# A planner that orders TensorE's work by a cost for every new division of the array, and new lengths for the units

## The chip, the cores and the metric

One core of one Trainium2 chip runs the kernel. The metric is the device time in microseconds (us) of the whole program. The median of three runs of the kernel before is 3766.3 us (3763.3 to 3766.73).

## The reference, cut to what matters

```python
x = x + tanh(g_xattn[0]) * L0_xattn(layernorm(x), ctx)      # 16 heads of 64, 1601 keys, batch 4 x 512 x 256
x = x + tanh(g_ffn[0])   * L0_ffn(layernorm(x))             # GQA attention (16 heads of 16), then MoE:
                                                            # 8 experts, top 2, capacity 1280, 256 -> 512 -> 256
x = x + tanh(g_xattn[1]) * L1_xattn(ctx, ctx, layernorm(x)) # queries layernorm(x), 16 heads of 16, masked, 1601 keys
x = x + tanh(g_ffn[1])   * L1_ffn(layernorm(x))             # attention (16 heads of 16) plus 8 dense experts, top 2
```

Every attention is an exact softmax: the row maximum is found first and subtracted, then the scores are exponentiated, then multiplied with the values, and divided by their sum.

## The kernel before, in words

All of the program's work is cut into units: one unit is a few matmuls of TensorE (PE) that fill one buffer of PSUM, and what evicts that buffer. Each engine walks through one common list of units in the same order and does its own share of each, waiting on counters of the others. So the list decides what stands behind what on every engine. PSUM has a ring of three buffers of two banks each (`RING = 3`), and two accumulators (`pv`) beside it. Nearly every unit takes one buffer of the ring; a score unit of the narrow blocks takes two.

The units that matter here, with the letters used below:

- **m**, a maximum: two matmuls of queries on 401 keys each (`maxa`, line 1075, for the wide first block with its heads of 64; `max3`, line 1173, for the third block). VectorE (DVE) reduces the buffer. In `max3` the head sits in 32 of the array's rows, and the next unit's head in the next 32.
- **x**, the same for the second and fourth block (`maxb`, line 1185): two heads, 512 keys each.
- **S**, scores of one tile of 124 keys. In the wide block (`scorea`, lines 1091 and 1094) one buffer, exponentiated by ScalarE (ACT), summed by GpSimd (POOL). In the third block (`scoreb`, lines 1205, 1212, 1218) two buffers: the mask is added by matmuls on all rows before and after, four heads stand in four groups of 32 rows, and the second pair of heads waits for the second buffer only when its turn comes. ACT exponentiates the two halves.
- **P**, exponentials times values into `pv` (`pva` line 1105, column halves of 64; `pvb` line 1233, four column groups of 32). No buffer of the ring.
- **u** and **o**, the sum over keys and the output projection of the wide block (`suma` line 1112, `outa` line 1120), with a chain of five DVE operations between them; **T**, transposes after a layer norm (line 1043); **K**, **V**, **Q**, projections (lines 1052 to 1067); **s**, **r**, **l** (`strip`, `rowb`, `low`, lines 1164 and 1192), one each for a group of four heads: r needs the reduction of all of the group's maxima on DVE.

The list is made on the host. Generators yield `Step`s, each with a length on PE (`pe`), the evictions (`use`), and the number of buffers (`slots`). `Pace` keeps a clock for PE, for each evicting engine and for the three buffers. `weave` merges the generators: it takes the step with the least progress among those that could start within `slack` of the first that could. There are three weaves: the wide block with the second one in it, the experts, and the third block with the fourth in it (called the last stretch below). Where the clocks leave PE idle near the ends, `warmed` puts dummy matmuls (line 1027). The scatter of the rows to the experts (`("scatter", b)`) has no `Step`: it goes into the list behind `ranks`, and POOL issues eight indirect DMAs there.

## Time and profile before

| | us |
|---|---|
| median of three runs | 3766.3 |
| the profiled execution, its own time | 3768.0 |
| its span, first to last instruction | 3766.0 |
| PE busy (share of the span) | 3496.2 (93%) |
| DVE busy | 1984.7 (53%) |
| ACT busy | 1442.6 (38%) |
| POOL busy | 986.3 (26%) |
| chain that ended last, share on PE | 85% |
| mean granted clock of TensorE | 0.956 |

Busy PE is time in which a matmul is under way; matmuls that wait inside a unit for a buffer can lie behind others that are still in flight, so a busy PE is not a full one. Idle time in brackets behind a row is that of the engine just before it, and the arrow names what ended it.

### The profile page before, as it was taken

What the parts mean: (1) busy time and instruction counts of PE and PEld (TensorE: products, weight loads), DVE (VectorE), ACT (ScalarE), POOL (GpSimd) and SP (SyncE); (2) the same over time, 40 slices, a digit from 0 to 9 for tenths busy, and PEclk for the clock granted to TensorE, in tenths of its full rate; (3) what the DMA queues carried; (4) which work ended last, traced back from release to release, by engine and by line L of the source; (5) the groups of instructions that cost most, each with busy time, mean ns of one, the idle gap of its engine ahead of it and who ended that gap; (6) DMA issues with size and microseconds to landing.
All of it is one profiled execution on the core that took longest, in us unless ns stands there. A gap on an engine that the chain in (4) does not pass through costs nothing.

```text
span 3766.0 us, 44527 instructions
## 1 busy us (share of the span) xinstructions
PE 3496.2 (93%) x18489; PEld 1465.0 (39%) x18489; DVE 1984.7 (53%) x3278; ACT 1442.6 (38%) x1645; POOL 986.3 (26%) x481
## 2 busy tenths in 40 slices
PE   7999999989999989999786949899999999999998
PEld 3444434434344443434235712234323422343252
DVE  4444456454554645555251156655666566656244
ACT  3333444434444334443231104443444244434513
POOL 3555355354544545454501030000000000000000
PEclk9999999999999989999898959999999999999999
DMA  3000000000000000000113320211101110110000
GB/s 147 12 12 29 12 6 12 12 35 12 7 12 8 28 23 6 12 2 8 73 32 109 118 56 23 65 27 39 28 23 28 39 28 23 28 39 22 7 13 6
DMA packets 68245, 114.87 MB, mean 31 GB/s; under 512 B 4850, under 2 KB 49546, under 8 KB 67531
## 3 DMA queue, kind: packets, MB, share of 16 engines
q1 hardware_dynamic: 62666, 97.08, 8.1%
q0 software_dynamic: 5376, 14.95, 1.8%
q8 instruction: 145, 2.38, 0.3%
q14 instruction: 58, 0.47, 0.0%
HBM read 101.79 MB, written 16.78 MB: 31 GB/s over the span
## 4 chain that ended last, share of the span: by engine, by line
PE 85%; DVE 7%; ACT 4%; POOL 2%; issue 2%; DMA 1%; another core or an unknown queue 0%; DVEq 0%; ACTq 0%; POOLq 0%
PE ring L1212 11%; PE pv L1105 10%; PE ring L1094 9%; PE pv L1233 9%; PE ring L1173 4%; PE ring L1205 3%; PE ring L1075 3%; PE ring L1218 3%; PE ring L1091 3%; PE ring L1052 3%; PE ring L1066 3%; PE ring L1067 2%; PE ring L1053 2%; PE ring L1291 2%; PE ring L1272 2%; PE ring L1120 2%
## 5 line engine op out<-in xcount | busy, mean ns | idle before, releaser
L1480 POOL TENSOR_TENSOR wide<-wide 124x1024 f32<-124x1024 f32 (+1 forms) x352 | 828.0, 2352 | 268.6 <-ACT wide L1374 254.7
L1381 ACT ACTIVATE wide<-ring 124x1024 f32<-124x1024 f32 (+2 forms) x544 | 530.3, 1023 | 620.2 <-PE ring L1212 615.8
L1374 ACT ACTIVATE wide<-ring 124x1024 f32<-124x1024 f32 (+1 forms) x416 | 425.9, 1025 | 582.3 <-PE ring L1094 547.0
L1615 DVE CUSTOM_DVE_ANT_0 rest<-ring,slim 128x802 bf16<-128x802 f32 x512 | 508.7, 994 | 265.2 <-PE ring L1173 217.3
L1599 DVE TENSOR_REDUCE max_a<-ring 128x2 f32<-128x802 f32 x512 | 508.1, 995 | 242.6 <-PE ring L1075 242.1
L1105 PE MATMUL pv<-wide 124*64 124x512 f32 (+1 forms) x1664 | 453.1, 624 | 25.2 <-ACT wide L1374 25.2
L1094 PE MATMUL ring<-wide 64*124 64x512 f32 (+1 forms) x1664 | 429.0, 594 | 0.0
L1625 DVE TENSOR_REDUCE slim<-ring 128x2 f32<-128x1024 f32 x256 | 309.7, 1223 | 159.2 <-PE ring L1185 156.5
L1212 PE MATMUL ring<-slim 32*128 32x512 f32 x2176 | 383.4, 651 | 5.0 <-DVE slim L1640 3.8
L1450 POOL DMA_DIRECT2D slim<-in_ctx_k x16 | 8.6, 542 | 1079.8 <-PE ring L1173 704.2
L1173 PE MATMUL ring<-slim 32*128 32x401 bf16 x1024 | 233.9, 356 | 38.1 <-DVE max_b L1615 13.2
L1477 POOL TENSOR_TENSOR wide<-wide 124x1024 f32<-124x1024 f32 x32 | 75.3, 2353 | 637.0 <-PE pv L1105 451.8
L1233 PE MATMUL pv<-wide,slim 124*32 124x512 f32 (+1 forms) x1664 | 224.3, 611 | 0.7 <-ACT wide L1381 0.6
L1212 PEld LDWEIGHTS ring<-slim 32*128 32x128 f32 x2176 | 128.5, 186 | 158.9 <-issue 99.4
L1105 PEld LDWEIGHTS pv<-wide 124*64 124x64 f32 (+1 forms) x1664 | 83.7, 136 | 264.9 <-issue 214.3
L1075 PE MATMUL ring<-wide 64*128 64x401 bf16 x1024 | 176.2, 341 | 7.1 <-DVE max_a L1599 5.8
L1091 PE MATMUL ring<-wide,select_b 64*128 64x512 bf16 x832 | 161.0, 384 | 14.1 <-ACT wide L1374 12.1
L1173 PEld LDWEIGHTS ring<-slim 32*128 32x128 bf16 x1024 | 55.7, 94 | 285.6 <-ACT wide L1381 137.1
L1094 PEld LDWEIGHTS ring<-wide 64*124 64x124 f32 (+1 forms) x1664 | 157.7, 186 | 22.3 <-issue 2.9
L1589 DVE CAST wide<-wide 128x800 bf16<-128x800 f32 x64 | 37.1, 579 | 244.5 <-ACT wide L1351 174.7
L1066 PE MATMUL ring<-wide 128*124 128x128 f32 (+1 forms) x832 | 160.1, 274 | 0.0
L1067 PE MATMUL ring<-wide 128*124 128x128 f32 (+1 forms) x832 | 159.5, 272 | 0.0
(236 smaller groups left out, 4120.0 us busy)
## 6 DMA issues: line engine op xcount, KB each, us to landing
slim<-in_ctx_k SPq DMA_DIRECT2D x16, 800.5 KB, 4.3
wide<-in_w_pair SPq DMA_DIRECT2D x32, 384.0 KB, 3.1
slim<-in_ctx_v SPq DMA_DIRECT2D x16, 744.0 KB
wide<-in_w SPq DMA_DIRECT2D x16, 512.0 KB, 4.9
wide<-in_we SPq DMA_DIRECT2D x16, 512.0 KB, 3.8
wide<-in_ctxT SPq DMA_DIRECT2D x4, 1601.0 KB, 7.6
slim<-in_ctx_k POOLq DMA_DIRECT2D x16, 400.2 KB, 4.7
wide<-padded_x SPq DMA_DIRECT2D x8, 640.0 KB, 6.5
```

The costliest lines, as they stand in the source:

```text
L1075: last = pe.matmul(slot[:, h * BANK:h * BANK + CHUNK], queries_ab[own, q * P:(q + 1) * P], keys_ab[own, c0:c0 + CHUNK], start=True, stop=True)
L1094: last = pe.matmul(slot[0:kn, h * BANK:(h + 1) * BANK], keys_a[own, p % 2, k0:k0 + kn], queries_a[own, p % 2, :], start=False, stop=True)
L1105: last = pe.matmul(pv_a[64 * h:64 * h + 64, :], values_a[0:kn, p % 2, k, 64 * h:64 * h + 64], exps_a[0:kn, slot_of["scorea", b, p, k], h * ...
L1173: last = pe.matmul(slot[:, j * BANK:j * BANK + CHUNK], queries_low(3, g)[own, q * P:(q + 1) * P], keys_low(3, g)[own, c0:c0 + CHUNK], star ...
L1212: last = pe.matmul(head_bank(unit, h), key_columns(blk, g, k0)[own, :], queries_place(blk, g)[own, :], start=blk != 3 or h >= 2, stop=blk ...
L1233: last = pe.matmul(pv_of[blk][PAD * h:PAD * h + PAD, :], value_columns(blk, g, k, kn, h), exps_tile(blk, b, g, k, h)[0:kn, :], start=k == ...
L1374: sc.activation(exps_a[0:kn, slot_of[unit], :], slot[0:kn, :], ACT.Exp, scale=WIDE ** -0.5).then_inc(scalar_done, 1)
L1381: sc.activation((exps_2 if blk == 2 else exps_34)[0:kn, first + 2 * i:first + 2 * i + 2, :].rearrange("p h n -> p (h n)"), ring_t[0:kn, ba ...
L1480: po.tensor_tensor(sums[0:kn, :], sums[0:kn, :], view, ALU.add).then_inc(pool_done, 1)
L1599: ve.reduce_max(max_a[:, :, q, c], slot.rearrange("p (h n) -> p h n", h=2)[:, :, 0:CHUNK], AX.X).then_inc(vector_done, 1)
L1615: ve.tensor_tensor_reduce(out=max_junk.rearrange("p (j n) -> p j n", j=2), in0=two[:, :, 0:CHUNK], in1=maskQ_sb[:, q, c0:c0 + 2 * CHUNK].r ...
L1625: ve.tensor_reduce(neg_cols[blk][:, q, 2 * hp * PAD:2 * hp * PAD + PAD + 1:PAD], slot.rearrange("p (h n) -> p h n", h=2), AX.X, ALU.max, n ...
```

## The change

The planner's `Step` gets the way in which its matmuls divide the array at its start and at its end (`parts`): 1 for all rows, 2 and 4 for groups of 64 and 32 rows, -2 and -4 for groups of columns. A step that starts in another division than the last one ended in can start `DIVIDE` = 0.13 later on PE's clock. Among the steps that are ready, one that needs a new division counts as further on by `alike`, 0 in the first two weaves and 0.05 in the last. The lengths of ten kinds of units are new, and `SLACK_1` is doubled. No instruction of any unit changes; only the order of the list does, with the choice of buffers and the number of dummy matmuls.

```diff
-SLACK_1 = 0.1
+SLACK_1 = 0.2
+DIVIDE = 0.13
+ALIKE_1 = 0.0
+ALIKE_3 = 0.05
...
 class Pace:
     def wish(self, step):
...
+        if at is not None and step.pe:
+            at = max(at, self.pe + self.turned(step))
         return at
+
+    def turned(self, step):
+        return DIVIDE if step.pe and step.parts[0] != self.parts else 0.0
...
     def accept(self, step):
         at = self.start(step)
+        if step.pe:
+            at = max(at, self.pe + self.turned(step))
...
-            self.pe = end
+            self.pe, self.parts = end, step.parts[1]
...
-        min((s for at, s in ready if at <= first + slack), key=Stream.progress).take(pace)
+        min((s for at, s in ready if at <= first + slack),
+            key=lambda s: s.progress() + (alike if pace.turned(s.step) else 0.0)).take(pace)
...
-                        yield Step(0.42, (("ve", 1.09),), 1, (("low", b, g),), ("max3", b, g, q, h, c))
+                        yield Step(0.35, (("ve", 1.09),), 1, (("low", b, g),), ("max3", b, g, q, h, c), parts=(4, 4))
...
-                yield Step(1.95 if blk == 3 else 1.0, (("sc", 1.02), ("sc", 1.02)), 2, (("rowb", blk, b, g),), unit,
-                           early=0.43 if blk == 3 else 0.0, gap=0.85 if blk == 3 else 0.3)
+                yield Step(2.0 if blk == 3 else 0.9, (("sc", 1.02), ("sc", 1.02)), 2, (("rowb", blk, b, g),), unit,
+                           early=0.43 if blk == 3 else 0.0, gap=0.85 if blk == 3 else 0.3,
+                           parts=(1, 1) if blk == 3 else (4, 4))
```

The other lengths: `maxa` 0.25 to 0.18, `scorea` 1.15 to 1.12, `pva` and `pvb` 0.97 to 0.86, `maxb` 0.28 to 0.23.

Counted on the list, dummy matmuls as division 1, PE goes to a new division between units 1211 times before and 1239 times after in the weave of the wide block, and 956 times before and 884 after in the last stretch. The dummy matmuls are 209 before and 218 after.

**Place 1**, PE, a group of heads in the last stretch, first batch. Before, one maximum (line 1173) follows each S (1205, 1212, 1218), then P (1233), then two maxima:

```order
L1212 MATMUL ring<-slim 128x512 x4
L1218 MATMUL ring<-slim,ident_b 128x512 x2
L1173 MATMUL ring<-slim 128x401 x2
L1233 MATMUL pv<-wide,slim 32x512 x4
L1173 MATMUL ring<-slim 128x401 x4
L1205 MATMUL ring<-slim,ident_b 128x512 x2
```

After (all lines are 16 higher), two maxima follow each S and two each P:

```order
L1228 MATMUL ring<-slim 128x512 x4
L1234 MATMUL ring<-slim,ident_b 128x512 x2
L1189 MATMUL ring<-slim 128x401 x4
L1249 MATMUL pv<-wide,slim 32x512 x4
L1189 MATMUL ring<-slim 128x401 x4
L1221 MATMUL ring<-slim,ident_b 128x512 x2
```

The cycle of five units (73 of them before, 3 after) becomes one of six (none before, 68 after, in 21 runs); the buffers are taken in turn so that S's first one is that of the second maximum and S's second one that of the third.

**Place 2**, DVE, end of the first such group. A maximum is two rows of line 1615 (before) or 1631 (after). Before, the four operations on P's finished sum (1709 to 1718) stand ahead of the group's last two maxima and of the reduction (1632) for which r waits:

```order
L1709 STREAM_TRANSPOSE rest<-raw_a 128x512
L1711 RECIPROCAL inverse<-rest 128x16
L1713 TENSOR_TENSOR rest<-rest,inverse 128x16x16
L1718 STREAM_TRANSPOSE wide<-rest 128x512
L1615 ISA rest,max_b<-ring,slim 128x802
L1615 ISA max_b 128x1
L1615 ISA rest,max_b<-ring,slim 128x802
L1615 ISA max_b 128x1
L1632 TENSOR_REDUCE slim<-max_b 128x4x4
```

After, the reduction (1648) comes first, while three of the group's P are still to come:

```order
L1648 TENSOR_REDUCE slim<-max_b 128x4x4
L1656 TENSOR_TENSOR slim<-ring,slim 128x512
L1662 CAST slim<-ring 128x512
L1773 SCALAR_TENSOR_TENSOR src<-wide,shares,src 128x256 x8
L1631 ISA rest,max_b<-ring,slim 128x802
L1631 ISA max_b 128x1
L1725 STREAM_TRANSPOSE rest<-raw_a 128x512
L1727 RECIPROCAL inverse<-rest 128x16
L1729 TENSOR_TENSOR rest<-rest,inverse 128x16x16
L1734 STREAM_TRANSPOSE wide<-rest 128x512
```

**Place 3**, PE, end of the first batch of the wide block. Before, u, T, o and then K:

```order
L1112 MATMUL ring<-wide,ones_f 64x512 x2
L1043 MATMUL ring<-consts,slim 128x128 x8
L1120 MATMUL ring<-wide 128x256 x4
L1052 MATMUL ring<-wide 128x401
L1053 MATMUL ring<-wide 128x401
```

After, P and T stand between u and o, and half of K too:

```order
L1128 MATMUL ring<-wide,ones_f 64x512 x2
L1121 MATMUL pv<-wide 64x512 x2
L1059 MATMUL ring<-consts,slim 128x128 x8
L1068 MATMUL ring<-wide 128x401
L1069 MATMUL ring<-wide 128x401
L1068 MATMUL ring<-wide 128x401
L1069 MATMUL ring<-wide 128x401
L1136 MATMUL ring<-wide 128x256 x4
```

At the end of the second batch o moves ahead of T altogether, with r, the layer norm and two S behind it; at the end of the third all of K, Q and V stand between T and o.

## Rows read from the trace of the kernel before

**Rows 1.** Busy time by stage: window, length, then PE, PEld, DVE, ACT, POOL, PEclk.
```profile
10.60:1982.20 1971.60, 1867.61 (x9942) 814.21 (x9942) 1020.92 (x1402) 786.20 (x918) 926.57 (x408) 0.97 0.07 22
2164.70:3766.00 1601.30, 1476.72 (x7892) 529.04 (x7889) 937.34 (x1821) 618.40 (x673) 39.14 (x47) 0.94 0.11 29
```

**Rows 2.** PE in order of time, wide block: start, length, engine, line, operation.
```profile
404.44 1.02 PE L1094 MATMUL ring<-wide 64*124 64x512 f32 x4
405.30 0.34 PE L1075 MATMUL ring<-wide 64*128 64x401 bf16 x2
405.56 1.08 PE L1105 MATMUL pv<-wide 124*64 124x512 f32 x4
```

**Rows 3.** All engines in order of time, one cycle of the last stretch.
```profile
2357.95 0.60 PE L1205 MATMUL ring<-slim,ident_b 124*128 124x512 bf16 x2
...
2358.80 0.08 DVE L1615 DVE_READ_ACCUMULATOR2_ANT max_b<- 128x1 f32 x1
2358.94 0.30 PEld L1212 LDWEIGHTS ring<-slim 32*128 32x128 f32 x4 [0.16 <-DVE max_b L1615]
...
2360.54 0.51 PE L1173 MATMUL ring<-slim 32*128 32x401 bf16 x2
...
2361.98 0.68 PE L1173 MATMUL ring<-slim 32*128 32x401 bf16 x4
...
2362.59 0.61 PE L1205 MATMUL ring<-slim,ident_b 124*128 124x512 bf16 x2
```

**Rows 4.** PE in order of time where S and P follow each other without maxima.
```profile
3573.94 0.61 PE L1205 MATMUL ring<-slim,ident_b 124*128 124x512 bf16 x2
...
3577.08 0.61 PE L1205 MATMUL ring<-slim,ident_b 124*128 124x512 bf16 x2
```

**Rows 5.** All engines in order of time, two maxima right behind an S.
```profile
2574.98 0.60 PE L1205 MATMUL ring<-slim,ident_b 124*128 124x512 bf16 x2
...
2577.12 0.51 PE L1173 MATMUL ring<-slim 32*128 32x401 bf16 x2
2577.67 0.99 DVE L1615 CUSTOM_DVE_ANT_0 rest<-ring,slim 128x802 bf16<-128x802 f32 x1 [0.82 <-PE ring L1173]
2577.82 0.51 PE L1173 MATMUL ring<-slim 32*128 32x401 bf16 x2 [0.19 <-ACT wide L1381]
...
2578.59 0.08 DVE L1615 DVE_READ_ACCUMULATOR2_ANT max_b<- 128x1 f32 x1
2578.81 0.99 DVE L1615 CUSTOM_DVE_ANT_0 rest<-ring,slim 128x802 bf16<-128x802 f32 x1
```

**Rows 6.** All engines in order of time, end of a group in the first batch.
```profile
2309.33 1.13 PE L1164 MATMUL ring<-slim,consts 128*128 128x512 f32 x2 [0.62 <-DVE max_b L1615]
2309.38 0.71 DVE L1709 STREAM_TRANSPOSE rest<-raw_a 128x512 f32<-128x512 f32 x1
...
2314.25 1.09 PE L1192 MATMUL ring<-consts,slim 128*128 128x128 f32 x4 [3.79 <-DVE slim L1632]
```

**Rows 7.** Groups of PE instructions by form: count, busy us, mean ns, idle before, its releasers.
```profile
L1205 PE MATMUL ring<-slim,ident_b 124*128 124x512 bf16 x384 | 120.3, 396 | 8.3 <-ACT wide L1381 4.0 <-DVE slim L1640 2.8 <-DVE slim L1625 0.9
...
L1120 PE MATMUL ring<-wide 128*128 128x256 f32 x256 | 68.3, 414 | 14.8 <-issue 9.4 <-DVE wide L1679 3.4 <-ACT wide L1346 2.0
...
L1192 PE MATMUL ring<-consts,slim 128*128 128x128 f32 x192 | 32.8, 299 | 19.7 <-DVE slim L1632 11.4 <-DVE slim L1625 7.8 <-ACT slim L1407 0.4
```

**Rows 8.** PE in order of time, the output unit between two batches of the third block.
```profile
2509.51 7.14 PE L1247 MATMUL ring<-slim,wide 128*128 128x256 f32 x32 [2.42 <-DVE wide L1718]
```

**Rows 9.** PE in order of time, end of the first batch of the wide block.
```profile
386.82 3.76 PE L1120 MATMUL ring<-wide 128*128 128x256 f32 x8 [4.25 <-issue]
```

**Rows 10.** Busy time in the stretch behind that stall, columns as in rows 1.
```profile
386.80:391.80 5.00, 4.98 (x11) 3.63 (x12) 1.18 (x1) 0.00 (x0) 0.00 (x0) 0.50 0.04 7
```

**Rows 11.** POOL and PE in order of time, behind the scatter of the third batch.
```profile
1809.71 7.32 POOL L1480 TENSOR_TENSOR wide<-wide 124x1024 f32<-124x1024 f32 x3
...
1817.08 1.98 PE L1112 MATMUL ring<-wide,ones_f 124*64 124x512 f32 x4 [13.05 <-POOL wide L1480]
```

More of the change, by code:

```diff
@@ L150, with __init__ @@
 class Step:
-    def __init__(self, pe=0.0, use=(), slots=0, needs=(), name=None, early=0.0, mark=None, late=0.0, gap=0.0):
+    def __init__(self, pe=0.0, use=(), slots=0, needs=(), name=None, early=0.0, mark=None, late=0.0, gap=0.0,
+                 parts=(1, 1)):
         self.pe, self.use, self.slots, self.needs, self.name = pe, use, slots, needs, name
-        self.early, self.mark, self.late, self.gap = early, mark, late, gap
+        self.early, self.mark, self.late, self.gap, self.parts = early, mark, late, gap, parts
 class Pace:
@@ L166, in __init__ @@
         self.ring = [0.0] * RING
-        self.done, self.picked, self.spare = {}, [], None
+        self.done, self.picked, self.spare, self.parts = {}, [], None, 1
     def start(self, step):
@@ L222, in progress, with weave @@
         return self.done / self.each - self.lead
-def weave(streams, pace, slack):
+def weave(streams, pace, slack, alike):
     while any(s.step for s in streams):
@@ L380, in wide_prep @@
                     for c in range(4):
-                        yield Step(0.25, (("ve", 1.0),), 1, (("qproj", b, p),), ("maxa", b, p, q, c))
+                        yield Step(0.18, (("ve", 1.0),), 1, (("qproj", b, p),), ("maxa", b, p, q, c), parts=(2, 2))
                         unit = emit(in_slot(("maxa", b, p, q, c), "vector"))
@@ L408, in wide_main @@
                     unit = ("scorea", b, p, k)
-                    yield Step(1.15, (("sc", 1.03),) + ((("po", 2.35),) if k else ()), 1,
-                               summed if k == 2 else (), unit, mark=0)
+                    yield Step(1.12, (("sc", 1.03),) + ((("po", 2.35),) if k else ()), 1,
+                               summed if k == 2 else (), unit, mark=0, parts=(2, 2))
                     in_slot(unit, "scalar")
@@ L419, in wide_main @@
                     unit = ("pva", b, p, k - 1)
-                    yield Step(0.97, (("sc", 0.6),) if k == NKT else (), 0,
-                               (("scorea", b, p, k - 1), ("vproj", b, p, 1)) + (summed if k == NKT else ()), unit)
+                    yield Step(0.86, (("sc", 0.6),) if k == NKT else (), 0,
+                               (("scorea", b, p, k - 1), ("vproj", b, p, 1)) + (summed if k == NKT else ()), unit,
+                               parts=(-2, -2))
                     emit(values_of(k - 1))
@@ L434, in wide_output @@
                 yield Step(0.95, (("ve", 2.9),), 1, (("pva", b, p, NKT - 1), ("scorea", b, p, NKT - 1, "all")),
-                           ("suma", b, p))
+                           ("suma", b, p), parts=(-2, -2))
                 unit = emit(on(in_slot(("suma", b, p), "vector"), *free["outT_a"]))
@@ L465, in slim_maxima @@
                     last = ("maxb", blk, b, g, q, hp)
-                    yield Step(0.28, (("ve", 1.23),), 1, (made,), last)
+                    yield Step(0.23, (("ve", 1.23),), 1, (made,), last, parts=(4, 4))
                     emit(on(in_slot(last, "vector"), *free[f"neg{blk}"]))
@@ L493, in slim_main @@
                 unit = ("pvb", blk, b, g, k - 1)
-                yield Step(0.97, (("sc", 0.6), ("ve", 2.3)) if k == tiles else (), 0, (("scoreb", blk, b, g, k - 1),) + valued +
-                           ((("outb", 3, b - 1),) if blk == 3 and b and k == tiles and g == 0 else ()), unit)
+                yield Step(0.86, (("sc", 0.6), ("ve", 2.3)) if k == tiles else (), 0, (("scoreb", blk, b, g, k - 1),) + valued +
+                           ((("outb", 3, b - 1),) if blk == 3 and b and k == tiles and g == 0 else ()), unit,
+                           parts=(-4, -4))
                 emit(on(unit, *pv_left))
@@ L670, in build_order @@
     weave([Stream(wide_main(), 220.9), Stream(wide_prep(), 150.9, MADE_1), Stream(wide_output(), 21.6, OUT_1),
-           Stream(each_batch(two_made), 21.9, MADE_2), Stream(each_batch(two_used), 43.4, USED_2)], pace, SLACK_1)
+           Stream(each_batch(two_made), 21.9, MADE_2), Stream(each_batch(two_used), 43.4, USED_2)], pace, SLACK_1, ALIKE_1)
     emit(*(on((f"load_{n}", e), *wide_done) for e in range(2) for n in ("up", "down")))
@@ L676, in build_order @@
     emit(*(on(("load_rows", e), *wide_done) for e in range(2)))
-    weave([Stream(experts_fill(wide_done), 156.0), Stream(masks_fill(slim_done), 1.0)], pace, SLACK_1)
+    weave([Stream(experts_fill(wide_done), 156.0), Stream(masks_fill(slim_done), 1.0)], pace, SLACK_1, ALIKE_1)
     emit(*(on(("gather", b), ("tensor", unit_of_last_down)) for b in range(B)))
@@ L685, in build_order @@
            Stream(each_batch(four_made), 33.6, MADE_4), Stream(each_batch(four_used), 37.2, USED_4),
-           Stream(each_batch(four_experts), 31.3, EXPERTS_4)], pace, SLACK_3)
+           Stream(each_batch(four_experts), 31.3, EXPERTS_4)], pace, SLACK_3, ALIKE_3)
 class Past:
```

## The prediction

> **What bounds the kernel now.** I read the busy time by stage first. The reader is to see two large stages: the wide block from 10.6 to 1982.2 us, with PE busy for 1867.6 of 1971.6, and the last stretch from 2164.7 us on, with PE busy for 1476.7 of 1601.3 [rows 1]. No other engine is near: DVE has 937.3 us of work in the last stretch and 1020.9 in the wide block. So PE sets the time, either by its own work or by what its next unit waits for. The second view is PE in order of time, for the price of a new division. Where a maximum follows an S of the wide block both stand in row groups of 64, and the next matmul starts (404.44 + 1.02 - 405.30) 0.16 us before the last ends; where P with its column groups follows the maximum, it starts only (405.30 + 0.34 - 405.56) 0.08 us before [rows 2]. The price of a new division is thus about 0.09 us when nothing else is waited for; the planner now believes 0.13. The third view is all engines in order of time within one cycle of the last stretch, for a wait that the page counts as busy time [rows 3]. The fourth is the idle time of groups of PE instructions, for the stalls that are not hidden [rows 6 to 11].
>
> **The change, part by part.** Nothing is added to any unit, so each term is a difference in order.
>
> *New divisions.* The wide block has 28 more (1239 against 1211), the last stretch 72 fewer (884 against 956). At 0.09 us that is +2.5 us in the wide block [rows 2]. In the last stretch the 6.5 us are contained in the price of the cycles below, and are not added again.
>
> The Trainium skill says under "TensorEngine Tiling (Array Packing)", section "Key Properties", that a change of the tiling mode, not merely of the tile, drains the array. The trace agrees, with 0.09 us for it. A drain of some 128 cycles, which "TensorE: Matmul & The Clock Gate" gives in its section on the phases of a matmul, would be an estimate of 0.05 us at 2.4 GHz, and 44 divisions fewer in all would be worth 2 us by it instead of 4.
>
> *The cycle of the last stretch.* Before: S starts at 2357.95; its second pair of heads starts only at 2358.94, when DVE has given back the second buffer (the accumulator is read out at 2358.80 for 0.08, and PE goes 0.06 later); the maximum starts 1.60 after that, at 2360.54; the pair of maxima behind P 1.44 later, at 2361.98; the next S 0.61 later, at 2362.59 [rows 3]. That is 0.99 + 1.60 + 1.44 + 0.61 = 4.64 us for one S, one P and three maxima. Without maxima, S and P take 3577.08 - 3573.94 = 3.14 us [rows 4], so a maximum costs (4.64 - 3.14) / 3 = 0.50 us, and four beside an S and a P would be worth 3.14 + 4 x 0.50 = 5.14 at that rate.
>
> After, four maxima stand in a cycle. For PE alone that is cheap: four matmuls of two maxima take 0.68 against 0.51 for one [rows 3], since the heads lie in different rows. But only three buffers exist. From rows 5: DVE starts 0.55 after a lone maximum does (2577.67 against 2577.12), starts the next 1.14 later (2578.81), has read out 1.00 after its start (2578.59 + 0.08), and PE follows 0.06 later. S takes as its first buffer that of the second maximum, which is free 0.55 + 1.14 + 1.00 + 0.06 = 2.75 us after the first maximum started. S takes as its second buffer that of the third maximum, which DVE reduces right behind, so that it comes free 1.14 after S's start, and the first maximum of the next cycle starts 1.60 later [rows 3]. The loop closes at 1.14 + 1.60 + 2.75 = 5.49 us. PE's own path in it is shorter: the second maximum has to wait for ACT until 2.84 after S's start (2577.82 - 2574.98) [rows 5], hence about 2.9, and 2.9 + 1.44 + 0.61 = 4.95. In the first cycle of a run nothing is late yet, and it costs about 5.0; the second about 5.3. The 68 cycles come in 21 runs; 21 are first, 15 second, 32 later: 21 x 5.03 + 15 x 5.29 + 32 x 5.49 = 361 us, against 68 x 5.14 = 350. **+11 us**; the ends are 68 x (4.64 + 0.17 - 5.14) = -22, if S's late half cost no more than now and the fourth maximum only its 0.17, and 68 x (5.49 - 5.14) = +24.
>
> The Trainium skill has a rule that speaks against this part: "TensorEngine Tiling (Array Packing)", section "PSUM Bottleneck", says that tiling makes TensorE faster and not the evacuation of PSUM, which may become the bound. In the present cycle DVE has 3 x 1.14 = 3.4 of 4.64 us to do and the rule doesn't yet bind; in the new one it has 4 x 1.14 = 4.6. By that rule alone the cycle would be 4.6 us; by the loop over three buffers it is 5.49, and the rival below takes it whole.
>
> *Ends of groups.* In the first batch s waits 0.62 and r 3.79 us, because DVE has the group's four closing operations ahead of the last two maxima (2309.38, against the start of s at 2309.33) [rows 6]. The reduction for which r waits accounts for 11.4 us of idle time over the program, which is 3 x 3.79 [rows 7]. After, it stands ahead of those operations, and S and P of the same group cover it: 3 x (0.62 + 3.79) = **-13 us**. What is late next there is the copy behind r (1640), for which the next S waits; S is now one of the old group, so this goes too. Between the first two batches the output unit waits 2.42 us for the transpose of the closing operations [rows 8], and the two S behind it belong to the 8.3 us of idle time of that line [rows 7]; the output unit now comes two S later. I take 2.4 and half of the 8.3: **-6 us** (bounds 0 and -11). At the end of the last stretch the fourth block stands alone, its units are S and P first and maxima last, and seven more dummy matmuls fill the gaps that the planner sees: 7 x 0.40 by the mean of another matmul of 512 columns [rows 7], **+3 us**, with 0 and +10 as bounds, as the maxima's reductions now have less beside them.
>
> *Ends of batches of the wide block.* Before, o stands right behind T and waits 4.25 us [rows 9], as DVE scales the layer norm first and then has its five operations for o. The idle time before that line is 14.8 us in all [rows 7]. After the first batch one K unit now stands in between; after the third, K, Q and V do; after the second, o is ahead of T. I let 10 of the 14.8 go. Behind the stall PE runs at a clock of 0.50, the level of 1.2 GHz, for at least 5 us [rows 10], which costs half of it, 2.5 us; two such stretches: -5. Against that, in the second batch the layer norm stands right behind o and r, its root is ahead of the next S's exponential on ACT, and P will wait for it; the price isn't in the trace, bounded by 0 and by the 4.25 of the stall it replaces, and I take the latter since the same chain is exposed. And 10 more r stand right behind an x: before, 30 of 32 stood behind a P, whose 1.08 us [rows 2] covered DVE; with an x instead, r may wait for a part of them, and with 0 and 1.08 as ends I take 0.4 each, nearer to 0 as x covers something too, +4 (0 to +11). Together -10 - 5 + 4 + 4 = **-7 us**.
>
> *The scatter.* It isn't in the planner's clocks, but costs most: behind it POOL starts on three adds that it owes only at 1809.71, and PE stands for 13.05 us [rows 11]. Three scatters lie in the wide block before and after. Two of them move from the end of a pair's S to its start, where POOL's adds of 2.4 us each (7.32 / 3) follow. ACT still waits for an exponential's buffer, two or three S later, for nearly as long. I cost it at **0**, with -8 and +8.
>
> *The sum.* +2.5 + 11 - 13 - 6 + 3 - 7 + 0 = -9.5 us. The profiled execution took 3768.0 us, 1.7 above the median of the runs; 3768.0 - 9.5 = 3758.5, and less the 1.7 it is 3757 for the median.
>
> **The rivals.** *The three buffers bind (slower).* One mechanism at one place: the loop of 5.49 us takes hold from the first cycle of each run, because DVE comes to it late (closing operations, x of the fourth block). Then the cycles cost +24 instead of +11, and the maxima that pile up behind S in mixed groups, 40 of the 68 cycles with x and fourth-block S between their runs, pay another 0.2 each, +8; the stalls at the ends of groups go only half, -6 and -3, and the rest stays: 2.5 + 32 - 9 + 3 - 7 = +21, time 3788. For it: the present cycle already waits for DVE inside S. Against it: 13 of the 21 runs have one or two cycles only. It decides from a mean cycle over 5.3. *Nothing to be seen.* The count of divisions hardly does what the change says, 44 fewer in 2167, 4 us; the stalls at batch ends come back in another place, and gains and losses cancel: 3763. For it: in the wide block cycles of two maxima, S and P have no wait that an order could take away. *The cycle is cheap (clearly faster).* S's second pair doesn't wait more than now, and the six-unit cycle takes 4.8: -22 instead of +11, time 3724. Against it: the loop above is closed with measured rows; a mean of 5.0 is more than I would bet on, 68 x (5.0 - 5.14) = -10, time 3736.
>
> **How the numbers follow.** Chances: the forecast 0.48, the slower rival 0.25, nothing to be seen 0.17, cheap cycle 0.10. What a measurement can tell from no change is 0.2%, 7.5 us, so 3758.8 is the border. The forecast of 3757 lies close to it, and its own range, 3742 to 3770 by the bounds of the terms, gives about 0.28 to faster, 0.15 to same and 0.05 to slower. With the rivals: faster 0.28 + 0.10 + 0.04 of the third case = 0.42; same 0.15 + 0.12 + 0.02 = 0.29; slower 0.05 + 0.01 + 0.23 = 0.29. The range that should hold it 8 times in 10 is 3732 to 3788.
>
> **What the profile after would show.** Right: cycles of S, two maxima, P, two maxima at 5.0 to 5.5 us, with S's second pair of heads about 1.1 us behind its start; no idle time of 3.8 before r in the first batch; under 6 us of idle time before line 1136 (now 1120); in the wide block the same cycle of two maxima, S and P. Wrong: a cycle under 4.9 or over 5.6; new stalls of several us in front of P in the wide block; a scatter that costs PE less than 5 or more than 14 us each. The forecast falls if the last stretch isn't 5 us shorter, give or take 10, or the wide block isn't about 4 us shorter.

## The result and the profile after

The changed kernel takes 3809.2 us (median of four runs, 3806.8 to 3810.5) against 3766.3 us: 1.0118 times as long, with an interval of 1.0104 to 1.0133. The forecast was 3757 us, with a range of 3732 to 3788. The profiled execution took 3808.8 us with a span of 3806.7, 40.7 longer than before. Of all executions behind the medians further down one alone stands apart: one of the twelve of run 11 took 7201.7 us, and that run's median is 3765.3 without it.

Busy time by stage of the changed kernel, columns as in rows 1: the wide block and the last stretch.

```profile
10.60:1995.40 1984.80, 1876.51 (x9936) 808.43 (x9944) 1020.06 (x1401) 784.32 (x918) 926.56 (x408) 0.97 0.07 22
2175.00:3806.70 1631.70, 1474.43 (x7888) 525.66 (x7896) 938.00 (x1821) 623.56 (x673) 39.27 (x47) 0.93 0.11 29
```

Against [rows 1] the wide block is 13.2 us longer and the last stretch 30.4 (the two stages between give back 3). In the last stretch PE is not busier; it waits 33 us more. The page of the profile puts 11% of the chain that ended last on DVE, 7% before:

```profile
PE 80%; DVE 11%; ACT 3%; POOL 3%; issue 2%; DMA 0%; DVEq 0%; ACTq 0%; POOLq 0%
```

Groups of PE instructions of the changed kernel by form, as in rows 7:

```profile
L1221 PE MATMUL ring<-slim,ident_b 124*128 124x512 bf16 x384 | 119.9, 395 | 44.5 <-DVE max_b L1631 37.3 <-ACT wide L1397 5.1 <-DVE slim L1641 0.6
L1136 PE MATMUL ring<-wide 128*128 128x256 f32 x256 | 64.2, 394 | 7.1 <-DVE wide L1695 6.6 <-issue 0.3
L1208 PE MATMUL ring<-consts,slim 128*128 128x128 f32 x192 | 31.3, 287 | 15.1 <-DVE slim L1641 14.7
```

The wait of S (8.3 us in [rows 7]) is 44.5 now, 37.3 of it for DVE's reductions of the third block's maxima. The output units of the wide block (14.8) and r (19.7) wait less, as forecast; but of r's 15.1 nearly all is now the wait for the reductions behind x, which was 7.8.

**The new cycle.** PE and DVE in order of time, one cycle of S, m, m, P, m, m, the answer to [rows 3]:

```profile
2277.58 0.60 PE L1221 MATMUL ring<-slim,ident_b 124*128 124x512 bf16 x2 [0.62 <-DVE max_b L1631]
...
2278.58 0.08 DVE L1631 DVE_READ_ACCUMULATOR2_ANT max_b<- 128x1 f32 x1
...
2280.32 0.62 PE L1189 MATMUL ring<-slim 32*128 32x401 bf16 x4
2280.87 0.99 DVE L1631 CUSTOM_DVE_ANT_0 rest<-ring,slim 128x802 bf16<-128x802 f32 x1 [1.05 <-PE ring L1189]
...
2282.01 0.99 DVE L1631 CUSTOM_DVE_ANT_0 rest<-ring,slim 128x802 bf16<-128x802 f32 x1
...
2282.93 0.08 DVE L1631 DVE_READ_ACCUMULATOR2_ANT max_b<- 128x1 f32 x1
2283.07 0.61 PE L1221 MATMUL ring<-slim,ident_b 124*128 124x512 bf16 x2 [0.63 <-DVE max_b L1631]
```

The loop closes as worked out: 2283.07 - 2277.58 = 5.49 us, 2.74 of them from S to the first maximum behind it and 2.75 through DVE's two reductions back to S. DVE itself is idle for 1.05 of it, and PE waits 0.63 at S: neither engine is full, and what binds is the way of the three buffers through both. The 68 cycles take 369.8 us, 5.44 in the mean.

**Batches of the last stretch.** Time from the first S of a batch to that of the next (the fourth: to its output unit), first before, then after:

```profile
2252.30:2520.00 267.70, 249.20 (x1369) 75.42 (x1368) 175.50 (x379) 119.26 (x126) 3.11 (x5) 0.97 0.15 40
2520.00:2888.00 368.00, 354.56 (x1912) 121.98 (x1913) 234.32 (x455) 150.48 (x164) 2.11 (x4) 0.96 0.11 27
2888.00:3259.40 371.40, 360.65 (x2002) 131.57 (x2002) 234.50 (x445) 153.42 (x167) 2.11 (x4) 0.98 0.11 28
3259.40:3600.70 341.30, 330.95 (x1829) 116.25 (x1825) 166.78 (x305) 150.32 (x163) 0.53 (x1) 0.94 0.09 25
```

```profile
2250.60:2510.20 259.60, 236.48 (x1354) 64.73 (x1353) 177.36 (x386) 120.02 (x124) 3.11 (x5) 0.99 0.14 38
2510.20:2911.80 401.60, 375.50 (x2001) 132.26 (x1998) 250.60 (x482) 154.18 (x166) 2.64 (x5) 0.94 0.11 28
2911.80:3299.10 387.30, 362.01 (x1953) 130.53 (x1949) 226.01 (x429) 154.59 (x166) 2.11 (x4) 0.94 0.11 29
3299.10:3643.60 344.50, 328.11 (x1811) 117.15 (x1808) 158.23 (x286) 150.44 (x163) 0.00 (x0) 0.94 0.07 21
```

The first batch is 8.1 us shorter, the second 33.6 and the third 15.9 longer, where the fourth block's units mix in; there the granted clock falls too, from 0.96 and 0.98 to 0.94. The stretch ahead of the first S hides a part of the loss: it took 87.6 us in the profiled execution of before and 75.6 after. DVE stood for 7.02 and 3.89 us there for something outside the engines, most likely a late transfer, and in all other runs that stretch takes 61 to 76 us. Five other executions with the old order of the last stretch took 1594.5 to 1609.2 us for it, and two others with the new one 1630.0 and 1633.9. So the new order costs 32 us in the mean of these, and from 21 to 39 us between single executions.

**The wide block** differs in two places. Its last output unit starts at 1861.2 us in both kernels; so all of the 13 us lie behind it, where the last batch of the second block runs alone, before and after:

```profile
1861.20:1981.60 120.40, 104.55 (x541) 40.77 (x541) 66.38 (x114) 43.28 (x49) 0.00 (x0) 0.97 0.21 73
```

```profile
1861.20:1995.00 133.80, 107.28 (x540) 41.67 (x548) 66.27 (x114) 43.12 (x49) 0.00 (x0) 0.89 0.18 65
```

Here x, r, S and P are those of the second block. The list had two x behind each P; now it has S and P in turn and then five x, one P among them, and eleven dummy matmuls. In order of time after:

```profile
1924.20 2.36 DVE L1641 TENSOR_REDUCE slim<-ring 128x2 f32<-128x1024 f32 x2 [7.36 <-PE ring L1201]
...
1928.79 3.45 DVE L1641 TENSOR_REDUCE slim<-ring 128x2 f32<-128x1024 f32 x3
1932.39 0.85 PE L1208 MATMUL ring<-consts,slim 128*128 128x128 f32 x4 [2.90 <-DVE slim L1641]
```

DVE stands idle for 7.36 us and then has five reductions within 8 us, three of them behind the four closing operations of P, with r behind them all: 21.9 us from one r to the next (1910.5 to 1932.4), where it was 18.0. Three r wait 2.9 us each in this way; before, none waited over 0.2. PE is idle for 26.5 us of the 133.8 (133.80 - 107.28), against 15.9 of the 120.4. Half clock adds to it: the granted clock is 0.89 here, 0.97 before.

Ahead of that last output unit gains and losses cancel, and one loss is large: pair 7 of the second batch (from its second value projection to that of the next pair) took 73.0 us and takes 89.6. gate2 of the first batch, two dozen small DVE operations, now stands amid POOL's adds. PE, DVE and POOL, after:

```profile
817.32 12.32 POOL L1496 TENSOR_TENSOR wide<-wide 124x1024 f32<-124x1024 f32 x5 [1.78 <-ACT wide L1390]
817.35 0.19 DVE L1518 TENSOR_REDUCE best<-prob 128x4 f32<-128x32 f32 x1
817.57 2.16 DVE L1520 TENSOR_TENSOR hit<-prob,best 128x32 f32<-128x32 f32 x1
...
820.21 2.02 DVE L1526 TENSOR_TENSOR pick<-hit,rstd 128x32 f32<-128x32 f32 x1
...
822.46 2.24 DVE L1798 TENSOR_SCALAR best<-best 128x4 f32<-128x4 f32 x1
...
824.95 2.26 DVE L1802 TENSOR_TENSOR both<-pick 128x32 f32<-128x32 f32 x1
...
827.45 2.23 DVE L1808 CAST chosen_b<-both 128x32 bf16<-128x32 f32 x1
...
831.90 0.52 PE L1091 MATMUL ring<-wide 64*128 64x401 bf16 x2 [6.63 <-DVE max_a L1615]
```

and before, in POOL's pause between two pairs:

```profile
797.31 0.19 DVE L1502 TENSOR_REDUCE best<-prob 128x4 f32<-128x32 f32 x1
797.53 0.19 DVE L1504 TENSOR_TENSOR hit<-prob,best 128x32 f32<-128x32 f32 x1
```

The same operation takes 0.19 or 2.16 us. Five are held until one of POOL's five adds (12.32 / 5 = 2.46 each) ends, 5 x 2.0 = 10 us, and PE's next maximum waits 6.63 for DVE. The Trainium skill says under "SBUF — State Buffer", section "Who interferes with whom", that a DVE instruction with two SBUF inputs, or a cast or scalar operation in a two-port mode, and a GpSimd instruction that reads SBUF block each other whole, and that a reduction never is blocked; the trace agrees (the reduction at 817.35 took 0.19 beside an add).

### The profile page after: what moved, and what is told of

Same layout as the page of the kernel before. It is cut to its first block, busy times and chain, and to the rows that moved or that the text cites. A ratio compares the mean times of both kernels' runs of the same rounds, so it can differ in the third digit from the quotient of the medians.

```text
span 3806.7 us, 44562 instructions
## 1 busy us (share of the span) xinstructions
PE 3500.2 (92%) x18480; PEld 1453.6 (38%) x18498; DVE 1984.5 (52%) x3278; ACT 1445.8 (38%) x1645; POOL 986.4 (26%) x481
## 4 chain that ended last, share of the span: by engine, by line
PE 80%; DVE 11%; ACT 3%; POOL 3%; issue 2%; DMA 0%; DVEq 0%; ACTq 0%; POOLq 0%
PE ring L1228 12%; PE pv L1121 9%; PE ring L1110 8%; PE pv L1249 8%; DVE rest L1631 4%; PE ring L1221 3%; PE ring L1234 3%; PE ring L1091 3%; PE ring L1082 2%; PE ring L1107 2%; PE ring L1189 2%; PE ring L1068 2%; PE ring L1083 2%; PE ring L1069 2%; DVE slim L1641 2%
## 5 line engine op out<-in xcount | busy, mean ns | idle before, releaser
L1397 ACT ACTIVATE wide<-ring 124x1024 f32<-124x1024 f32 (+1 forms) x544 | 536.1, 1023 | 671.8 <-PE ring L1228 662.7
L1390 ACT ACTIVATE wide<-ring 124x1024 f32<-124x1024 f32 (+1 forms) x416 | 425.9, 1025 | 625.5 <-PE ring L1110 575.4
L1228 PE MATMUL ring<-slim 32*128 32x512 f32 x2176 | 397.8, 667 | 9.0 <-ACT wide L1397 4.3
L1189 PE MATMUL ring<-slim 32*128 32x401 bf16 x1024 | 198.3, 363 | 23.9 <-DVE max_b L1631 16.1
L1107 PE MATMUL ring<-wide,select_b 64*128 64x512 bf16 x832 | 161.9, 386 | 13.0 <-ACT wide L1390 10.2
L1221 PE MATMUL ring<-slim,ident_b 124*128 124x512 bf16 (+1 forms) x416 | 130.0, 395 | 44.7 <-DVE max_b L1631 37.5
```

The costliest lines, as they stand in the source:

```text
L1189: last = pe.matmul(slot[:, j * BANK:j * BANK + CHUNK], queries_low(3, g)[own, q * P:(q + 1) * P], keys_low(3, g)[own, c0:c0 + CHUNK], star ...
L1228: last = pe.matmul(head_bank(unit, h), key_columns(blk, g, k0)[own, :], queries_place(blk, g)[own, :], start=blk != 3 or h >= 2, stop=blk ...
L1390: sc.activation(exps_a[0:kn, slot_of[unit], :], slot[0:kn, :], ACT.Exp, scale=WIDE ** -0.5).then_inc(scalar_done, 1)
L1397: sc.activation((exps_2 if blk == 2 else exps_34)[0:kn, first + 2 * i:first + 2 * i + 2, :].rearrange("p h n -> p (h n)"), ring_t[0:kn, ba ...
```

## The experiments

Stage lengths are of each run's profiled execution: wide block from 10.6 us to the last ranks matmul, last stretch from the last expert matmul to the end of the span. That execution can lie off the median: by 22.6 us below it in run 2, 10.3 below in run 7, 10.2 above in run 12. The ratio is to the executions of before that stood beside a run. Runs 1 to 4 are of one chip, 5 to 8 of a second, 9 to 12 of a third, 13 and 14 of a fourth; before took 3762.8 to 3766.7 us beside them, so medians of different groups compare to some 4 us.

| kernel | median us | ratio to before (95%) | wide block | last stretch |
|---|---|---|---|---|
| before | 3766.3 | | 1971.6 | 1601.3 |
| after | 3809.2 | 1.0118 (1.0104-1.0133) | 1984.8 | 1631.7 |
| 1 wide new, last old | 3781.1 | 1.0036 (1.0023-1.0048) | 1987.8 | 1600.2 |
| 2 last: lengths only | 3794.7 | 1.0079 (1.0057-1.0101) | 1984.6 | 1595.6 |
| 3 before, scatter held | 3745.5 | 0.9949 (0.9937-0.9961) | 1952.6 | 1597.6 |
| 4 after, scatter held | 3787.5 | 1.0059 (1.0046-1.0073) | 1964.2 | 1630.0 |
| 5 before, gate2 and ranks in pauses | 3731.9 | 0.9912 (0.9898-0.9926) | 1942.8 | 1597.4 |
| 6 after, half reduction | 3697.5 | 0.9825 (0.9810-0.9840) | 1990.5 | 1515.8 |
| 7 before, half reduction | 3687.0 | 0.9803 (0.9789-0.9817) | 1969.5 | 1513.4 |
| 8 before, price in the last stretch | 3867.2 | 1.0282 (1.0260-1.0305) | 1970.1 | 1698.3 |
| 9 after, gate2 and ranks in pauses | 3780.5 | 1.0054 (1.0039-1.0069) | 1961.0 | 1633.9 |
| 10 one maximum each | 3824.5 | 1.0168 (1.0151-1.0185) | 1943.5 | 1687.6 |
| 11 lengths, small slack | 3765.8 | 1.0009 (0.9997-1.0022) | 1941.5 | 1630.0 |
| 12 wide without the price | 3752.1 | 0.9967 (0.9954-0.9981) | 1961.4 | 1609.2 |
| 13 the same, ranks held | 3717.7 | 0.9877 (0.9860-0.9894) | 1931.5 | 1594.5 |
| 14 last lengths again | 3744.6 | 0.9942 (0.9922-0.9961) | 1939.9 | 1619.2 |

**1 and 2.** The last stretch by old rules; and by new lengths without the price.

```diff
-DIVIDE = 0.13                       # 1: and the old lengths of blocks 3 and 4
-ALIKE_3 = 0.05                      # 2: the new lengths stay
+DIVIDE, DIVIDE_3 = 0.13, 0          # DIVIDE_3: in the last weave
+ALIKE_3 = 0
```

> The wide block planned by the new rules, the last stretch by the old ones (its old lengths, no price for a division, nothing for alike). Theory: the two stretches lose independently of each other, 13.2 us in the wide block and 27.4 us in the last stretch by the two traces, so this kernel takes 3809.2 - 27.4 = 3782 us, with a last stretch of 1601 +- 3 us. Rival: the last stretch is longer because of the state in which the planner's clocks enter it; then it stays well above 1601 us and the time above 3790.

Met: 3781.1, last stretch 1600.2. The two stretches lose independently of each other.

> The changed kernel without the price of a division and without alike in the last stretch; the new lengths stay. The order there has 83 cycles of S, m, P, m, m again and none of S, m, m, P, m, m. Theory A, the price of the division makes the loss there: about as split, 3782 us, and down to 3775 since ten more good cycles stand in it. Theory B, the shorter lengths (a maximum at 0.35) do it, because they make the stream that makes the maxima look late: 3800 us or more.

Neither theory: the profiled execution was the fastest of six, 3772, with a last stretch 4.6 us shorter than in run 1, but the others reached 3804. Time follows the granted clock from execution to execution: 3772.0 at 0.957, 3790.8 at 0.952, 3804.0 at 0.948. By the medians the new lengths alone cost 13.6 us in the last stretch (3794.7 - 3781.1), and the price with `ALIKE_3` the other 14.5 (3809.2 - 3794.7).

**3 and 4.** The scatter held back.

```diff
-        emit(("scatter", b))
+        held.append(b)              # the fourth is emitted at once
...
+                    if k == NKT - 1 and held and (b, p) != (B - 1, PAIRS - 2):
+                        emit(("scatter", held.pop(0)))
```

> The kernel before, with one thing changed: the scatter of the first two batches goes into the list right behind the last S of the pair of heads during which it falls due, that of the third batch behind the very last S of the wide block. POOL then has its pause of some 20 us between two pairs' sums in front of it. Theory: the stalls of 10.1, 8.8 + 1.8 and 13.05 us behind the scatters go, and with them most of the half clock behind them: 3766 - 25 to - 40, so 3726 to 3741 us. Rival: other waits (o behind the layer norm, ACT) stand right behind and take over: 3756 or more.

> The changed kernel with the same delay of the scatters. Theory: POOL's ten us of scatter are what the stalls of 8.5 + 3.7, 8.2 and 8.7 us wait for; they go: 3809 - 20 to - 35, so 3774 to 3789 us, and the wide block then differs from that of the kernel before with held scatters by less than 8 us. Rival: the stall of 6.6 us in front of it, for DVE, is the one that counts in the pair of heads where the change lost most, and the loss stays: the wide block is still 13 us longer than with the old order and held scatters.

Gains of 18.6 us (the runs of before beside it took 3764.0) and 21.7 us: the first is 4.5 us short of its range, the second within it. In 3 the DVE operations of ranks now meet POOL's adds, and four in each of the three batches take 1.9 to 2.3 us. 4 keeps 11.6 us of the wide block's loss, more than the 8 allowed: the scatter alone is not its cause.

**5 and 9.** gate2 and ranks made to wait for the last S of a pair; in 9 one pair later for gate2, since it is ready later there.

```diff
-(("turn", 20, b),), ("gate2", b))
+(("turn", 20, b),) + pause(b, PAIRS - 3), ("gate2", b))   # 9: PAIRS - 2
-(("gate2", b),), ("ranks", b))
+(("gate2", b),) + pause(b, PAIRS - 1), ("ranks", b))
+    def pause(b, p):
+        return (("scorea", b + 1, p, NKT - 1),) if b + 1 < B else ()
```

> The kernel before, with gate2 and ranks (with the scatter behind it) of the first three batches made to wait until the last S of a pair of heads stands in the list, so that DVE's small operations and POOL's eight indirect DMAs both fall into POOL's pause between two pairs. Theory: a small DVE operation that meets one of POOL's adds is held until that add ends (0.19 us becomes 2.2; in the changed kernel five times in gate2 of the first batch, 817.6 to 829.7 us), and the scatter holds back POOL's adds; with both in the pause neither happens, and the time is below that with only the scatters held, 3745: 3730 to 3742 us, the small operations all at 0.2 us. Rival: the DVE work and the scatter now delay the sum and the output unit of that pair, 5 us each time: 3750 or more.

Met: 3731.9. One or two operations of a batch's ranks are still held (2.2 to 2.4 us), none of gate2's.

> The changed kernel with gate2 of the first three batches held until the last S of the next pair of heads but one of the batch, and ranks with the scatter until the last S of the batch, so that both fall into POOL's pauses. Nothing else. Theory: of the 13 us that the wide block lost, all and more hang on the place of gate2 in the first batch (five small DVE operations of 0.2 us that POOL's adds stretch to 2.0 to 2.3 us) and of the scatter; then the wide block, 1984.9 us now, comes within 5 us of the 1942.8 of the kernel before with gate2 and ranks in the pauses, and the whole takes 3764 to 3775 us. Rival: many small places lose (m right before o, r behind x), and the new wide block stays 10 us or more above it: 1953 or more, 3780 or more.

The rival holds. Pair 7 of the second batch falls from 89.6 to 61.4 us. With the scatter alone held (run 4) it takes 81.7, so 20.3 us of it are the DVE operations of gate2 and ranks amid POOL's adds (with the old order, where gate2 stood in the pause, the same step from run 3 to run 5 is 7.0); but the wide block stays 18.2 above run 5's: 7.5 behind the last output unit (133.9 against 126.4), 8.2 in the 89.4 us ahead of it, with a new stall of 6.74 before an S, and 2.7 in the 31 pairs before.

**6 and 7.** DVE reduces 401 of 802 keys; the other half is left out of the maximum.

```diff
-ve.tensor_tensor_reduce(out=..., in0=two[:, :, 0:CHUNK], ..., scalar=-3e38, ...)
+ve.tensor_tensor_reduce(out=..., in0=slot[:, 0:CHUNK], ..., scalar=30.0, ...)
```

> The changed kernel; in the third block DVE reduces only the first 401 of a maximum's 802 keys, with a floor of 30 for the maximum (the other half is left out of the maximum; all scores are still computed). DVE's 0.99 us become about 0.5. Theory A, the loop over three buffers through DVE sets the cycle of S, m, m, P, m, m: it falls from 5.44 to 4.6 +- 0.2 us, and the last stretch comes within 6 us of that of the kernel before with the same half reduction. Theory B, TensorE's own work or the order of divisions sets it: the cycle stays over 5.2 and the last stretch stays 25 us longer than that of its counterpart.

> The kernel before with the same half reduction of the third block's maxima (the second half of the keys is left out of the maximum). Its cycle of S, m, P, m, m waits for DVE too, inside S (0.99 us instead of 0.6 or so): from 4.64 to about 4.25 us by theory A, so 73 x 0.4 = 29 us less and some at mixed cycles: 3725 to 3740 us. By theory B it stays at 3760.

S of three cycles in 6 (PE in order of time):

```profile
2270.86 0.61 PE L1221 MATMUL ring<-slim,ident_b 124*128 124x512 bf16 x2
...
2275.59 0.60 PE L1221 MATMUL ring<-slim,ident_b 124*128 124x512 bf16 x2
...
2280.33 0.60 PE L1221 MATMUL ring<-slim,ident_b 124*128 124x512 bf16 x2
```

Theory A: the cycle takes 4.74 us instead of 5.49, with no wait at S, and the last stretches come within 2.4 us of each other, where 30.4 lay between them. A reduction repeats at 0.73 us here and is read out 0.58 after its start, so the same loop would close at 0.73 + 1.60 + (0.55 + 0.73 + 0.58 + 0.06) = 4.25 us. That is below PE's own path of 4.95 in the prediction: the buffers no longer bind. Batch by batch the agreement is less close: against run 7 the first batch is 8.6 us shorter in run 6, the second still 21.1 longer (369.8 against 348.7) and the third 7.5 shorter. So the second batch loses by more than the time of the reductions. Both fell further than I had put it (7 to 3687), since mixed units and group ends wait for DVE too, and PE is at half clock less: 136 and 139 us of the last stretch instead of 219 and 194.

**8.** The price alone, old lengths.

> The kernel before, with nothing but the price of 0.13 for a new division in the last stretch (old lengths, nothing for alike, wide block as before). Divisions there fall from 956 to about 830, and the order has S, m, m, m, P, m, m 34 times with plain S, P cycles between. Theory A, maxima in heaps are dear because only three buffers take them and DVE needs 1.14 us for each: the last stretch is 25 to 60 us longer than before, time 3790 to 3825. Theory B, fewer divisions are a gain or nothing and only the lengths were wrong: 3755 to 3768.

Worse than either: +101 us. A cycle of S, m, m, m, P, m, m, PE in order of time:

```profile
2264.37 0.60 PE L1224 MATMUL ring<-slim,ident_b 124*128 124x512 bf16 x2 [0.64 <-DVE max_b L1634]
...
2267.11 0.62 PE L1192 MATMUL ring<-slim 32*128 32x401 bf16 x4
2268.30 0.51 PE L1192 MATMUL ring<-slim 32*128 32x401 bf16 x2 [0.56 <-ACT wide L1400]
...
2271.01 0.60 PE L1224 MATMUL ring<-slim,ident_b 124*128 124x512 bf16 x2 [0.64 <-DVE max_b L1634]
```

It takes 6.64 us here, with two waits, and 6.95 in the mean of 34, against 3.14 + 5 x 0.50 = 5.64 at the rate of [rows 3, 4], and PE is at half clock for 324 us of the last stretch. Its list has the fewest divisions of all, 821.

**10 and 11.** Wide block of run 5, `SLACK_3 = 0.3`; in 11 also no price.

> Wide block of the kernel before with gate2 and ranks in the pauses; last stretch by the changed kernel's rules, but with SLACK_3 = 0.3 instead of 0.5: the list then has 106 cycles of S, m, P, m and none of S, m, m, P, m, m. Theory: the heaps of maxima are the fault and not the price of divisions; a maximum that finds its buffer costs 0.50 us wherever it stands, so the cycle takes 3.14 + 2 x 0.5 = 4.15 us and the last stretch 1580 to 1595 us as with the old rules: 3720 to 3736 us in all. Rival: more divisions (960) and less air in the cycle cost as much as the heaps, last stretch 1610 or more, 3750 or more.

My theory fell, by 88 us. The cycle is cheap, 4.06 us in the mean of 106. But a group has 32 maxima and 13 S, and two in a cycle are too few: the rest stand in a heap at the group's end, PE in order of time:

```profile
2262.18 0.68 PE L1195 MATMUL ring<-slim 32*128 32x401 bf16 x6
2266.35 0.85 PE L1195 MATMUL ring<-slim 32*128 32x401 bf16 x2 [3.49 <-DVE max_b L1637]
2267.50 0.85 PE L1195 MATMUL ring<-slim 32*128 32x401 bf16 x2 [0.30 <-DVE max_b L1637]
...
2276.66 2.08 PE L1186 MATMUL ring<-slim,consts 128*128 128x512 f32 x2 [0.29 <-DVE max_b L1637]
```

Nine maxima follow at DVE's pace of 1.15 us with nothing beside them, at half clock (0.85 instead of 0.5 us for a pair of matmuls). The first batch takes 339 us instead of 271 (run 5).

> The same wide block; last stretch with the new lengths, no price for a division, SLACK_3 = 0.3: 103 cycles of S, m, P, m, m. Theory: these cost 4.63 us each as in the last stretch with the new lengths alone (83 of them there), fewer plain cycles stand between, and the last stretch takes 1575 to 1590 us where TensorE's clock is not granted less: 3715 to 3730 us. Rival: with DVE at 3.4 of 4.63 us for so long, the ends of groups wait for it and the clock falls more often: 1600 us or more.

The rival holds: 1630. The cycles are as good as forecast (4.69), but the fourth block falls behind: the fourth batch and what follows take 569 us instead of 500 (run 5).

**12.** No price in the wide block (`DIVIDE = 0`), last stretch as in run 1.

> New lengths and SLACK_1 = 0.2 in the wide block, but no price for a division anywhere; last stretch by the old rules. Beside the first experiment (the same with the price in the wide block, 3781 us, wide block 1987.8 us) only the price in the wide block differs. In this list gate2 of the first batch stands in POOL's pause again, and behind the last output unit of the wide block the second block's last batch has one maximum pair behind each P instead of five maxima and eleven dummy matmuls at a group's end. Theory: the price's order loses in these two places; from the last output unit to the ranks it takes 120 to 124 us instead of 133.8, the wide block 1965 to 1975 us, and the whole 3758 to 3769 us. Rival: the new lengths and the doubled slack make the loss and the price little: the wide block stays at 1980 us or more, 3774 or more.

Better than the theory: 29 us below run 1, and 14.6 below before (3766.7 beside it). Pair 7 of the second batch takes 65.8 us. From the last output unit on it takes 128.5, not 120 to 124 (run 1: 137.6). So in the wide block the new lengths with the doubled slack are a gain of 14.6 us, and the price a loss of 29.

**13 and 14.**

> The kernel of the run before (new lengths and SLACK_1 = 0.2 in the wide block, no price, last stretch by the old rules, 3752 us), with ranks and the scatter held until the last S of the batch. gate2 stays where it is, in POOL's pause already. Theory: the scatter still costs the wide block some 15.6 - 5 and 12.8 - 5 us of waits in the pairs (1, 7) and (2, 7), and some of the 6.5 of (3, 6); held, these go: 3725 to 3737 us, wide block 1935 to 1948 us. Rival: new lengths and held ranks take away the same stalls, and the time is that of the kernel before with both held, 3732, or above: 3738 or more.

3717.7, below the forecast: the gains nearly add, 14.6 (run 12) and 33.8 (run 5) against 45.4 under the 3763.1 of before beside it. It is the fastest of all that reduce every key.

> Wide block of the kernel before with gate2 and ranks in the pauses (3732 us in all with the old last stretch), last stretch with the new lengths and no price, as in the second experiment, whose single executions lay between 3772 and 3804 us. Theory: the new lengths alone cost nothing in the last stretch as long as TensorE's clock is granted as before (profiled last stretch 1589.6), but its order, with fewer plain cycles, meets the half clock more often, by chance; executions between 3727 and 3760 with a span that follows the granted clock, median 3735 to 3750. Rival: the order itself is as good as the old one and the spread was of that chip: all within 3725 to 3740.

Met: executions from 3732.1 (clock 0.960) to 3753.6 (0.954), median 3744.6, which is 12.7 above run 5; run 2 was 13.6 above run 1. So the new lengths alone cost some 13 us in the last stretch. Their second and third batches are shorter (725 us together, run 5: 746), the fourth and what follows longer (543 against 500).

## Why the prediction was wrong, step by step

The prediction had the last stretch 5 us shorter and the wide block 4.5 us shorter; they are 30.4 and 13.2 us longer. The terms one by one:

*New divisions* (+2.5). Too small to see: the rows give 0.16 - 0.08 = 0.08 us a change rather than 0.09, and run 8, with the fewest divisions, is the slowest of all. What the planner does to save a division decides. By the medians its price costs 29 us in the wide block (runs 1 and 12) and, with `ALIKE_3`, 14.5 in the last stretch: together the whole loss of 43. The new lengths gain 14.6 there and lose 13.6 here.

*The cycle* (+11). The mechanism was right and the size short, and this is the first step that failed. Later cycles took 5.49 as worked out, but first ones 5.21 instead of 5.03 and second ones 5.64 instead of 5.29, since DVE comes late to them: 369.8 us for the 68, +20 instead of +11 by the same rate. The slower rival named this (a mean over 5.3) and priced the whole at 3788; runs 6 and 7 show the mechanism.

*Ends of groups* (-13) held in kind: s and r in the first batch no longer wait, since the reduction stands where it was said to:

```profile
2307.31 0.19 DVE L1648 TENSOR_REDUCE slim<-max_b 128x16 f32<-128x32 f32 x1
...
2309.74 0.60 PE L1208 MATMUL ring<-consts,slim 128*128 128x128 f32 x4
```

Only 8.1 us are left as the first batch's whole gain, as its cycles lose, and a wait of 3.77 us for the layer norm's root on ACT is new before a P at 2441.05. *Output unit* (-6): it waits 1.09 instead of 2.42 [rows 8], the line 1.9 instead of 4.1; the half of S's 8.3 that I let go became 44.5. *The tail of the last stretch* (+3) is 2.4 us shorter.

*Ends of batches* (-7): after the first batch o waits 0.76 instead of 4.25 [rows 9] and the pair is 5.2 us shorter, as said, and the line of the output units waits 7.1 instead of 14.8 (the prediction had named under 6). The P behind the layer norm's root waits 0.34 us, for which I had 4.25. The r behind x, for which I had 0.4 us each and 4 in all, wait 8.9 us in the wide block instead of 0.2, and not evenly: three r of the last batch take 2.9 each, above the 1.08 that was my upper bound for one. *The scatter* (0) was right as a difference: 8.5 + 3.7, 8.2 and 8.7 us of stalls where there were 10.1, 8.8 and 13.05 [rows 11].

What failed above all is the sum: every place that I had not priced stood in it as zero. In the last stretch these are the second and third batch, +33.6 and +15.9, where maxima stand in heaps beside the fourth block's units too; I had 0.2 us a piece for that, in the rival alone. In the wide block it is the tail, +13.4, whose order I had not looked at, as I had for the fourth block's; and gate2's place, by which pair 7 of the second batch is 16.6 us longer and uses up the gains of other pairs. Lost to the clock, (1 - clock) x time over the four batches of the last stretch, are 50.6 us before and 70.6 after by the rounded clocks shown above, 46.1 and 71.7 by the unrounded ones. So at most some 20 to 26 of the 44.6 us by which they are longer are half clock. It comes with the waits (with the half reduction the difference goes, 136 and 139 us at half clock), and I had counted it as a gain at one place and nowhere as a loss. Not shown: how the loss in the second and third batch divides between heaps and the order of the fourth block's units, though run 6 leaves the second batch 21.1 us longer than run 7, so the reductions are not all of it. Nor did a run part the price from `ALIKE_3`, or the new lengths of the wide block from `SLACK_1`. Also open is why the new lengths alone lengthen the fourth batch.

## What to carry to other kernels

A planner that charges for one resource moves its work onto the resource that it models too kindly: price the eviction loop (here three buffers and 1.14 us of DVE for each maximum) before the switch of 0.08 us. Give an evicting engine its work at the pace that the deadline needs, neither in heaps nor too thin: 32 maxima over 13 scores want two and a half each. And in a changed order look at the stretches where a stream runs alone, and at what small operations of one engine now stand beside on another.

## What the runs showed of the hardware that was not expected

- A DVE operation of 0.16 to 0.19 us on 4 or 32 columns takes 1.9 to 2.4 us when it meets one of POOL's adds of 2.46 us; the reduction beside an add at 817.35 took 0.19.
- The mean granted clock of one program varies between executions, and its time with it: 3772.0 us at 0.957 and 3804.0 at 0.948 for the same list (run 2), 3.6 us for 0.001 of the clock. The kernel of run 13 stayed between 3714.5 and 3722.1, at 0.962 to 0.963.
- Two matmuls of 401 columns that take 0.51 us take 0.85 at half clock, in a stretch of run 10 where PE waited for DVE between every two.
